# Query transposes in another bank, the residual loaded in the last stage, an early ranks' table and four sum buffers, in a transformer layer with 64 experts

## The reference, cut to what matters

```python
x = x + _layernorm(_L0_attn_ref(_layernorm(x), ...))
x = x + _layernorm(_L0_ffn_ref(_layernorm(x), ...))

# attention: softmax over the 16 heads of one token, not over tokens
cq = h_t @ Wc + bc
q = concat(cq @ Wcq + bcq, cq @ Wqr + bqr)       # 16 heads of 32 + 16
ckv = h_t @ Wckv + bckv
k = concat(ckv @ Wck + bck, h_t @ Wkr + bkr)     # 16 heads of 32 + 16
v = ckv @ Wv + bv
scores = jnp.einsum('bsid,bsjd->bsij', q, k) * SCALER
out = jnp.einsum('bsij,bsjd->bsid', softmax(scores), v) @ Wo + bo

# feed-forward: 64 experts, 6 for each token, at most 128 tokens an expert
scores = softmax(xf @ gate_w.T); topk_w, topk_idx = top_k(scores, 6)
gu = einsum('ech,ehi->eci', xp[buf_tok], gate_up_proj)
eo = einsum('eci,eih->ech', silu(g) * u, down_proj) * buf_w[..., None]
routed = zeros.at[buf_tok].add(eo)
shared = silu(xf @ shared_gate_w.T) * (xf @ shared_up_w.T) @ shared_down_w.T
```

## Time and profile before

| | us |
|---|---|
| median of 3 executions (range) | 2183.13 (2182.82 to 2186.1) |
| the profiled execution | 2195.51 |
| its span, first to last instruction | 2193.7 |
| stage one, to the first load of stage two | 0 to 1493.6 |
| stage two, to the landing of the last scatter | 1493.6 to 2009.1 |
| stage three | 2009.1 to 2193.7 |
| PE busy | 1944.4 (89%) |
| DVE busy | 1428.8 (65%) |
| ACT busy | 1089.3 (50%) |

### The profile page before, as it was taken

How to read it: one execution, slowest core, us unless ns; L and a number is a source line. 1 busy time by engine, 2 the same in 40 slices (tenths; PEclk the granted TensorE clock), 3 DMA queues, 4 the chain that set the end, 5 groups by cost and what they waited for, 6 DMA issues and landing times. The chain is left out here.

```text
span 2193.7 us, 48888 instructions
## 1 busy us (share of the span) xinstructions
PE 1944.4 (89%) x14529; PEld 1527.0 (70%) x14529; DVE 1428.8 (65%) x3872; ACT 1089.3 (50%) x1745; POOL 527.0 (24%) x773
## 2 busy tenths in 40 slices
PE   6899999999999999999999999864888888887997
PEld 4788888888888888888888888752444444444775
DVE  6677777777777777777777777643333333333775
ACT  4656566666666666666666666521222222222443
POOL 1111111111111111111111111111333333332776
PEclk8999999999999999999999999976899988897999
DMA  5344444444444444444344444346999989996774
GB/s 170 77 130 109 129 109 129 109 129 109 129 109 129 108 128 109 128 109 130 108 128 109 128 109 124 91 132 196 254 266 277 263 252 256 266 265 174 265 264 185
DMA packets 400560, 350.41 MB, mean 160 GB/s; under 512 B 288192, under 2 KB 296896, under 8 KB 400448
## 3 DMA queue, kind: packets, MB, share of 16 engines
q1 hardware_dynamic: 380992, 296.21, 46.6%
q0 software_dynamic: 14336, 35.66, 7.3%
q10 hardware_dynamic: 5184, 17.96, 2.0%
HBM read 216.01 MB, written 133.73 MB: 159 GB/s over the span
## 5 line engine op out<-in xcount | busy, mean ns | idle before, releaser
L576 ACT COPY qT<-bank 48x512 f32<-48x512 f32 x256 | 269.1, 1051 | 147.5 <-PE bank L429 142.8
L839 POOL TENSOR_SCALAR ve<-mv 128x1 f32<-128x1 f32 x192 | 44.9, 234 | 1152.5 <-DVE mv L676 1152.5
L576 ACT COPY kT<-bank 48x512 f32<-48x512 f32 x256 | 268.2, 1048 | 5.0 <-PE bank L429 0.3
L1073 PE MATMUL e_gu<-w,xgT 128*128 128x384 f32 x512 | 204.2, 547 | 1.0 <-ACT xgT L1152 1.0
L436 PE MATMUL bank<-wgu,xfT 128*128 128x416 f32 x512 | 183.6, 359 | 1.4 <-ACT xfT L576 1.4
L437 PE MATMUL bank<-wgu,xfT 128*128 128x416 f32 x512 | 182.6, 357 | 0.0
L1318 POOL DMA_INDIRECT acc_scratch<-eo,sidx x64 | 101.5, 1587 | 302.3 <-DVE gate L1234 171.7
L625 ACT ACTIVATE prob<-prob 128x512 f32<-128x512 f32 x128 | 78.7, 633 | 175.4 <-DVE prob L767 175.4
L1230 DVE COPY sidx<-idx 128x1 int32 (+1 forms) x64 | 9.8, 154 | 231.5 <-DMA acc_scratch<-eo,sidx 231.3
L453 PEld LDWEIGHTS score_ps<-kT,qT 48*64 48x64 f32 x4096 | 131.9, 137 | 35.7 <-issue 35.7
L693 DVE SCALAR_TENSOR_TENSOR th<-th,bank 128x192 f32<-128x192 f32 x128 | 45.3, 354 | 168.9 <-ACT th L612 162.9
(11 more groups left out here) (177 smaller groups left out, 4831.2 us busy)
## 6 DMA issues: line engine op xcount, KB each, us to landing
w<-w_eg SPq DMA_DIRECT2D x64, 768.0 KB
w<-w_ed SPq DMA_DIRECT2D x64, 384.0 KB
xf_scratch<-xf SPq DMA_DIRECT2D x64, 288.0 KB, 2.1
acc_scratch<-zero SPq DMA_DIRECT2D x65, 256.0 KB, 4.1
xin<-x SPq DMA_DIRECT2D x64, 256.0 KB, 3.1
v_scratch<-v SPq DMA_DIRECT2D x64, 256.0 KB, 3.5
vbd<-v_scratch SPq DMA_DIRECT2D x128, 128.0 KB, 3.2
o_scratch<-o SPq DMA_DIRECT2D x256, 64.0 KB, 2.3
```

The lines of the kernel that those rows point to most:

```text
L576: nc.scalar.copy(dst, src).then_inc(done.sem, 1)
L1073: last = nc.tensor.matmul(gu_ps[par], xgT[:, par, n, :], w1[:, place, n, :], start=(n == 0), stop=(n == KD - 1))
```

## The change

- **Banks.** The second half of the queries' transposes goes into `b7`, the output product's bank, instead of `b6`, the keys'. The wait for `d_k` moves from the head of the iteration to the value product, the wait for the copied queries (`a_qT`) from the value product to the gate product into `b7`; a wait for `d_y` is added.
- **Hand-over.** The first experts' weights are loaded an iteration earlier. The ranks' table has memory of its own; its first 62 rows are loaded in stage one's iteration NT+3 and the last two after its last iteration. Constants and the triangle are kept, no longer loaded again.
- **Sums' buffers.** `eo` and `sidx` have four buffers. Copy and index wait for scatter j-5 (`added.at(j - 1 - NW)`), no longer for j-3.
- **Residual.** It is no longer loaded beside the weights, but in the ring of stage three, eight groups ahead like the hidden rows and now the routed sums too. All three, and the raw `w_sd`, have memory of their own; the first eight hidden and residual groups follow the last weights without a wait.

```diff
+        all_ranks = sb("all_ranks", [NT, E, P], BF16)
...
+            def load_ranks(a, b):
+                sp.dma_start(all_ranks[a:b].rearrange("n e t -> n (e t)"),
+                             rank_d[a:b].rearrange("n e t -> n (e t)")).then_inc(ranks_in, 16)
...
-                if isinstance(i, int) and i == NT + 2:
+                if isinstance(i, int) and i == NT + 1:
                     sp.wait_ge(pe_k.sem, pe_k.at(NT - 1))
                     for e in range(NW):
                         load_expert(sp, e, e)
+                if isinstance(i, int) and i == NT + 3:
+                    for n in range(2):
+                        sp.wait_ge(rank_out[n].sem, rank_out[n].at(NT - 4 + n))
+                    load_ranks(0, NT - 2)
             pipeline(sp, iteration)
+            for n in range(2):
+                sp.wait_ge(rank_out[n].sem, rank_out[n].at(NT - 2 + n))
+            load_ranks(NT - 2, NT)
...
-                    pe.wait_ge(d_k.sem, d_k.at(i - 2))
                     turn(q, pe_qT, 0, b3)
                 if active(i - 2):
-                    turn(q, pe_qT, 1, b6)
+                    pe.wait_ge(d_y.sem, d_y.at(i - 4))
+                    turn(q, pe_qT, 1, b7)
...
                     pe.wait_ge(a_latT.sem, a_latT.at(i - 1))
+                    pe.wait_ge(d_k.sem, d_k.at(i - 2))
+                    product(b6, [latT[:, 1 - par, :, 1, :]], [wv[:, :, 0, :]], d_latT, i - 1, pe_v)
+                if active(i - 4):
+                    pe.wait_ge(a_xfT.sem, a_xfT.at(i - 4))
                     pe.wait_ge(a_qT.sem, a_qT.at(i - 2))
-                    product(b6, [latT[:, 1 - par, :, 1, :]], [wv[:, :, 0, :]], d_latT, i - 1, pe_v)
...
-            sp.dma_start(rank[:].rearrange("n e t -> n (e t)"), rank_d.rearrange("n e t -> n (e t)")).then_inc(start, 16)
-            sp.dma_start(ident, cst[:, C_ID:C_ID + P]).then_inc(start, 16)
-            sp.dma_start(c[:], cst[:, C_IOTA:C_END]).then_inc(start, 16)
-            sp.dma_start(eo[:, 0, 0:P], cst[:, C_TRI:C_TRI + P]).then_inc(start, 16)
...
-                    if with_x1 and u % (NW // GROUPS) == 0:
-                        load_group(r * GROUPS + (EARLY - GROUPS) + u // (NW // GROUPS))
...
+            sp.dma_start(wsd_raw[:], w_sd.rearrange("(c p) n -> p c n", p=P)).then_inc(wsd_in, 16)
+            for u in range(NR):
                 load_hidden(u, u)
+                load_residual(u, u)
             sp.wait_ge(added.sem, added.at(E - 1))
-            for u in range(NA):
+            for u in range(NR):
                 load_routed(u, u)
...
+                    load_hidden(g + NR, u)
                     sp.wait_ge(g_sum.sem, g_sum.at(g))
                     settle(sp)
-                    load_routed(g + NA, u)
+                    load_routed(g + NR, u)
+                    sp.wait_ge(out_done[u].sem, out_done[u].at(g))
+                    settle(sp)
+                    load_residual(g + NR, u)
...
-                    act.wait_ge(added.sem, added.at(j - 3))
-                    nc.scalar.copy(eo[:, 1 - par, :], out_ps).then_inc(ea_out.sem, 1)
+                    act.wait_ge(added.sem, added.at(j - 1 - NW))
+                    nc.scalar.copy(eo[:, (place - 1) % NW, :], out_ps).then_inc(ea_out.sem, 1)
```

More of the change, by code:

```diff
@@ L597, in iteration @@
                     act.wait_ge(pe_qT.sem, pe_qT.at(i - 2, 2))
-                    spread(qT, b6, a_qT, 1)
+                    spread(qT, b7, a_qT, 1)
                 if active(i - 4):
@@ L902, in experts_and_norm @@
         mhalf = sb("f_mhalf", [P, G])
-        with ExitStack() as searched:
-            rank = searched.enter_context(nc.sbuf_tensor("e_rank", [NT, E, P], BF16))
-            xg = searched.enter_context(nc.sbuf_tensor("xg", [P, NW, D + E], F32))
         wsd = sb("wsd", [P, 2, SI // P, D], F32R)
+        wsd_raw = sb("wsd_raw", [P, SI // P, D])
         hT = sb("f_hT", [P, G, 2, SI // P, P], F32R)
-        NH, NA = 8, NW
-        w1_flat, w2_flat = w1[:].rearrange("p w c n -> p w (c n)"), w2[:].rearrange("p w c n -> p w (c n)")
-        wsd_raw = w1_flat[:, 0].rearrange("p (c n) -> p c n", n=D)
-        hid_in = [w1_flat[:, (1 + u // 2) % NW, u % 2 * G * SI:(u % 2 + 1) * G * SI] for u in range(NH)]
-        acc = [w2_flat[:, u] for u in range(NA)]
+        NR = 8
+        hid_rows = sb("f_h", [P, NR, G * SI])
+        acc = sb("f_acc", [P, NR, G * D])
+        res = sb("f_res", [P, NR, G * D])
         hT_ps = [ends_ps, rowsT_ps]
         sh_ps = gu_bank
-        start = ctx.enter_context(nc.semaphore("start"))
         setup = ctx.enter_context(nc.semaphore("setup"))
@@ L951, in experts_and_norm @@
         ready = ctx.enter_context(nc.semaphore("f_ready"))
-        h_in = [groups(f"f_h_in{n}", 16, NH, n) for n in range(NH)]
-        acc_in = [groups(f"f_acc_in{n}", 16, NA, n) for n in range(NA)]
-        out_done = groups("f_out", 16)
+        h_in = [groups(f"f_h_in{n}", 16, NR, n) for n in range(NR)]
+        acc_in = [groups(f"f_acc_in{n}", 16, NR, n) for n in range(NR)]
+        res_in = [groups(f"f_res_in{n}", 16, NR, n) for n in range(NR)]
+        out_done = [groups(f"f_out{n}", 16, NR, n) for n in range(NR)]
         p_hT = tiles("f_p_hT")
@@ L986, in ring @@
         def ring(eng, body):
-            for u in range(NH):
+            for u in range(NR):
                 body(u, u)
-            with eng.Fori(1, NG // NH - 1) as r:
-                for u in range(NH):
-                    body(r * NH + u, u)
-            for u in range(NH):
-                body(NG - NH + u, u)
+            with eng.Fori(1, NG // NR - 1) as r:
+                for u in range(NR):
+                    body(r * NR + u, u)
+            for u in range(NR):
+                body(NG - NR + u, u)
         def rows(ap, t):
@@ L1029, in load_hidden, with load_residual @@
             def load_hidden(g, u):
-                sp.dma_start(hid_in[u], rows(group(h_d), g)).then_inc(h_in[u].sem, 16)
+                sp.dma_start(hid_rows[:, u], rows(group(h_d), g)).then_inc(h_in[u].sem, 16)
+            def load_residual(g, u):
+                sp.dma_start(res[:, u], rows(group(x1_d), g)).then_inc(res_in[u].sem, 16)
             def load_routed(g, u):
-                sp.dma_start(acc[u % NA], rows(group(acc_d[0:T, :]), g)).then_inc(acc_in[u % NA].sem, 16)
-            for u in range(NH):
-                if u < NH - 2:
-                    sp.wait_ge(e_gu.sem, e_gu.at(E - NW + 1 + u // 2))
-                else:
-                    sp.wait_ge(wsd_lo, 1)
+                sp.dma_start(acc[:, u], rows(group(acc_d[0:T, :]), g)).then_inc(acc_in[u].sem, 16)
@@ L1040, in _ @@
+            sp.dma_start(wsd_raw[:], w_sd.rearrange("(c p) n -> p c n", p=P)).then_inc(wsd_in, 16)
+            for u in range(NR):
                 load_hidden(u, u)
+                load_residual(u, u)
             sp.wait_ge(added.sem, added.at(E - 1))
-            for u in range(NA):
+            for u in range(NR):
                 load_routed(u, u)
             def refill(g, u):
-                if not isinstance(g, int) or g + NH < NG:
+                if not isinstance(g, int) or g + NR < NG:
@@ L1058, in _ @@
         def _(pe):
-            pe.wait_ge(start, 64)
-            pe.wait_ge(setup, 1)
-            nc.tensor.matmul(ends_ps[0:NT, 0:E], tri, rank[:, :, P - 1], start=True, stop=True).then_inc(setup, 1)
+            pe.wait_ge(ranks_in, 32)
+            nc.tensor.matmul(ends_ps[0:NT, 0:E], tri[0:NT, 0:NT], rank[:, :, P - 1], start=True, stop=True).then_inc(setup, 1)
             def of(ap, e):
@@ L1176, in normalise, with store @@
                 for n in range(G):
-                    dst = acc[u % NA][:, n * D:(n + 1) * D]
+                    dst = acc[:, u, n * D:(n + 1) * D]
                     nc.scalar.activation(dst, dst, ACT.Identity, bias=shift[:, u % 2, n:n + 1],
                                          scale=rstd[:, u % 2, n:n + 1]).then_inc(a_norm.sem, 1)
-            def store(g):
+            def store(g, u):
                 act.wait_ge(g_sum.sem, g_sum.at(g))
                 settle(act)
-                src = res[:, g, :] if isinstance(g, int) else res[:, bass.ds(g, 1), :].rearrange("p g n -> p (g n)")
-                act.dma_start(rows(group(out), g), src).then_inc(out_done.sem, 16)
+                act.dma_start(rows(group(out), g), res[:, u]).then_inc(out_done[u].sem, 16)
             def body(g, u):
```

101 lines of the change are left out of this document (38 added, 63 removed).

## The result

The changed kernel takes 2203.61 us (median; 2195.4 to 2220.84), the kernel before took 2189.63 on the same chips (2181.46 to 2203.84). The ratio is 1.0068, with a 95% interval of 1.0051 to 1.0085: slower by 0.7%, where 2160 us was forecast, faster by 1%. The forecast started from the 2183.13 us of the first three executions of the kernel before; over 20 executions its median is 6.5 us higher, so of the 43.6 us between forecast and result 37 are the change's and 6.5 the starting point's. The profiled execution took 2210.38 us with a span of 2208.6, against 2193.7 before.

The account below looks back on a forecast made before the run. Bounds: a norm chain through DVE and POOL in stage one, the scatters in stage two, a POOL-ACT loop in stage three. 0 + 18 - 53 + 8 + 4 = -23 gave 2172.5 profiled, 2160 us median; range 2125 to 2190.

Parts of the forecast that it names:

- Four sum buffers: Stage two: DVE's and ACT's waits for the scatter go, the scatters' own order stays; term 0.
- the 6.7: Stage two: the forecast scatter period in us without residual loads, in place of 7.72.
- Residual out of stage two: Stage two: without residual loads 52 scatter periods shorten from 7.72 to 6.7 us, -53 us.
- rival 3: Stage two: buffers and fewer loads bring scatters to the engines' floor of 6.16 us, -28, 2132 us; chance 0.11.
- Rival 4: Stage two: scatters lengthen by weight loads always in flight; slower from a 7.14 us period, 2202 us at 7.5; chance 0.13.
- sample of 6.81: Stage two, trace before: scatters from 1944.29 to 1971.54, without residual loads, took 6.81 us each.
- Weights ahead of the last `oin`: End of stage one: eight weight loads queued earlier delay the last `oin` transposes, +10.8 us.
- The ranks' table: Hand-over to stage two: 62 rows over two engines take 18.4 to 26.6 us; together with the early weights +18 us.
- Rival 1: Hand-over: the 62 rows spread over all engines, +1 in place of +18, 2143 us; chance 0.20.
- Banks: Stage one: the queries' stall shrinks from 1.15 us to 0.5, that of `xf` grows from 0.43 to about 1.1; term 0.
- Rival 2: Stage one: the queries' stall is what bounds a tile, -39 us more, 2121 us; chance 0.06.
- End of stage two and stage three: Residual burst beside the last scatters, +8 us; stage three's groups with more bytes at 340 GB/s, +4 us.

Follow-up runs that it names:

- e2: The changed kernel with two sum buffers again, all else as changed; 2183.68 us, ratio 0.9993 to the kernel before.
- e6: e5 with two sum buffers again in place of four; 2156.72 us, ratio 0.9866 to the kernel before.
- e13: e8 with four sum buffers in place of two; 2136.12 us, ratio 0.978 to the kernel before.
- e3: The changed kernel with the ranks' table loaded as 48 and 16 rows instead of 62 and 2; 2181.29 us, ratio 0.9954 to the kernel before.
- e5: e3 with the first experts' weights loaded behind the last `oin` again; 2162.24 us, ratio 0.9881 to the kernel before.
- e1: The kernel before with the banks' part of the change alone; 2188.64 us, ratio 1.0007.
- e8: e6 with the probabilities' sum on DVE moved ahead of the first normalisation; 2119.29 us, ratio 0.9697 to the kernel before.
- e9: e8 with the banks of the kernel before; 2144.99 us, ratio 0.9807 to the kernel before.
- e7: e5 with each weight load also waiting for a scatter's landing, four sum buffers kept; 2176.49 us, ratio 0.9959 to the kernel before.
- e10: e8 with the weights of expert j+4 loaded only after the first product of expert j+2; 2132.65 us, ratio 0.9756 to the kernel before.
- e11: e8 with `w1` loaded earlier, after expert j+2's rows are transposed, and `w2` at its old place; 2119.87 us, ratio 0.9688 to the kernel before.
- e12: e8 with weight loads after the first four experts cut to 16 columns, so its output isn't the layer's; 2053.03 us in one execution.

## Why the prediction was wrong

**Four sum buffers: the step that failed.** It said "Term 0 by itself; it evens out what the 6.7 assumes". In the runs it costs 0.58 us a period in this pair of profiles (e2), 0.12 and 0.39 in the two other pairs (e6, e13), 0.37 between the means of the two groups, and 16 to 20 us of time where the pairs are clear of the noise. The reasoning held that the scatters' order sets the pace and PE's lead changes nothing. The first half is right (49 of 52 scatters wait for a landing). But a scatter's length isn't fixed: it is 4.9 us alone and up to 10.3 beside loads, and with two sum buffers the loads fell on a scatter's start about half as often as with four. In the kernel before the same tie shows: its loads come 4.1 us after a scatter's start in the median, 19 of 52 within 0.1 us of that; in the kernel after 1 of 53. That the buffers are the cause is shown by the pairs; that they act through the loads' moment explains about half of it and is otherwise argued. The 9.33 and 5.00 of the earlier trace rows already said that the length depends on what runs beside a scatter; I put it down to how much runs, and not to when.

**Residual out of stage two: right mechanism, the gain halved by its neighbour.** With two buffers the period is 6.90 us (e2), 43 us less than before over 52 periods, where 6.7 and -53 were forecast. The engines' floor of 6.16 (rival 3) was not reached in either. With the four buffers it is 7.48, and 12.5 us are left.

**Rival 4 came in**, at almost its own number (7.5 us, 2202 us; measured 7.48, 2203.61), beyond its threshold of 7.14. That the time fits within 2 us is luck: the hand-over was 15 us worse than forecast and the starting point 6.5 us off, and the mark that varies between executions, the first scatters and stage three took back 19. It named PE's lead of two experts as the cause. Its picture of loads "always in flight" doesn't fit: the DMA engines became idler, 0.86 against 0.92. The loads come at more scattered moments, not always. I gave it 0.13, because the sample of 6.81 spoke against it; but that sample is of the kernel with two buffers, and says nothing about four.

**Weights ahead of the last `oin`: right.** +10.8 forecast, +11.4 measured. A part of it is in the issues themselves, 8.44 us for four, a place I had not named (e2 and e3, with the weights early too, have one issue of 6.6 and 6.1 us there; e5, with them late, none).

**The ranks' table: right cause, mis-sized.** The two items together were put at +18, they cost +33.2 (13.8 up to the rank write, 19.4 behind it). The second step that failed is the rate in it: 18.4 to 26.6 us for the 62 rows over two engines, from 19.1 to 27.6 GB/s an engine. The load took about 36 us: 1.02 MB in the 35.3 us of the stretch, on two engines, are 14.4 GB/s each. The rate could have been read in the trace of the kernel before: the 64 packets of 16 KB of the same table took 1.18 us each there, so 31 of them one after the other, an engine's half of the 62, take 37 us by that. After the change they took 1.06 us each, two at a time. That there are two engines shows in the stretch's busy share, 0.14, near 2 / 16 = 0.125, and 48 rows make the delay go away (e3). The Trainium skill (DMA: Bandwidth & Descriptors, "Why a DMA increments its semaphore by 16 and not by 1") gives two engines for 62 rows; the trace agrees, with that 0.14. Rival 1, all engines, is refuted.

**Banks: right.** Term 0 forecast, 0 measured (e1), a tile 22.0 us, the wait for `xf` 1.04 us in the iteration shown. Rival 2 is refuted as stated, and e8 and e9 show the reason given to be the right one: with the sum's 1.2 us out of the norm's chain the same banks bring 26 us.

**End of stage two and stage three.** +8.9 for a forecast of +8. Stage three -2.5 for +4: a group keeps its period (POOL's sums in the timeline lie 5.43 us apart before and 5.34 after), with the DMA engines 0.97 busy at 369 GB/s. My 340 GB/s, the rate of a stretch at 0.77 busy scaled up, was too low.

**The sum.** Terms 0 + 18 - 53 + 8 + 4 were -23; the spans give 0 + 33.2 - 12.5 + 8.9 - 2.5 = +27.1, and with -8.6 for the mark that varies between executions and -3.7 for the first two scatters +14.8. Of the 37.8 us between the two sums 40.5 are the period's (30 of them the buffers', by e2) and 15.2 the hand-over's. The medians differ by 14.0; how much of the 8.6 averages out over the executions was not taken apart.

**What stays open.** That the load's moment relative to the scatter is what costs is the reading that fits most of the table of periods and e7, but it accounts for about half of the difference between two and four buffers, the deliberate shift (e10) brought only a third of what it implies, and splitting the burst (e11) nothing. What within the DMA engines lengthens a scatter that starts with a load was not seen. The granted clock of PE over the 52 periods is lower in the kernel after (0.88 against 0.96 in e2), and over the kernels it goes with the period (0.93 to 0.97 with two buffers, 0.88 to 0.93 with four). It isn't what sets the period: e7 has the same 7.47 us at 0.94, and the scatters start at a landing, not at PE's pace. How far it is more than a result of PE's waits was not separated.

## What to carry to other kernels

Where a chain of transfers one after the other sets the pace, an extra buffer ahead of it can't speed it up, and it can slow it by cutting the tie that kept other transfers off it: ask of every wait that is removed what it also kept in time. The longest stall isn't always the one that bounds: if another wait on the same engine takes its time up at once, shorten that other chain first and then remove the stall (here nothing alone, 26 us after the other). And look at the number of rows of a large load on the path: 62 instead of 48 cost 25.9 us here.

## What the runs showed of the hardware

- A load of 62 rows of 16 KB ran on two of 16 engines at 14.4 GB/s each, about half of what an engine gives in the best slice of the trace (27.6), and the next load of the table was issued 35.8 us after the last rank write. With 48 rows first (e3) that was 7.9 us; the 48 rows landed 8.5 us after issue.
- Issues behind eight large loads in SP's queue slow down themselves: four `o_scratch` issues took 8.44 us instead of 2.62.
- An adding scatter of 128 rows of 2 KB lands after 4.9 us in the median with hardly any loads beside it (e12). With 1.18 MB of loads to each it is 5.8 to 6.1 us in the four kernels with two buffers of the sums and 6.2 to 7.1 in the four with four.
- In stage three the 16 engines moved 369 GB/s at a busy share of 0.97.
